# Values projected with the tokens on the partitions and moved by DMA, their weighting moved from VectorE to GpSimd, and the input normalisation moved ahead

## The reference, cut to what matters

```python
def layer(x, txt):                      # 32 images of 3x96x96, 32 texts of 32x256
    z = layernorm(patches(x)) @ W_proj  # 36 patches of 768 values -> 256
    h = concat([cls, layernorm(z)]) + pos
    h = concat([h, txt], axis=1)        # 32 x 69 tokens x 256
    n = layernorm(h)
    q, k, v = n @ q_w + q_b, n @ k_w + k_b, n @ v_w + v_b      # 16 heads of 64
    attn = softmax(q @ k.T / 8)                                # 69 x 69 each
    h = h + concat(attn @ v) @ l_w.T + l_b
    return h + moe(layernorm(h))        # top 2 of 8 experts, each 256 -> 1024 -> 256, capacity 690
```

## Time and profile before

| | |
|---|---|
| time, median of 3 runs | 701.84 us (701.57 to 702.82) |
| profiled execution: time, span | 701.51 us, 699.7 us |
| busy PE / DVE / ACT / POOL | 681.5 / 505.0 / 296.1 / 276.6 us |
| stage A until about | 48 us |
| stage B, first `context` to last | 58.58 to 397.34 us |
| finishing the routing, first fetch | until 422.7 us |
| stage D until about | 692.7 us for PE |

### The profile page before, as it was taken

The page is one execution under the profiler, slowest core; times in us unless marked ns, Lnnn a source line. Parts: engine busy times, 40 slices in busy tenths (PEclk is TensorE's granted clock), DMA queues, the critical chain, the costliest instruction groups (busy, mean ns, idle before and its releaser), DMA issues.

```text
span 699.7 us, 16960 instructions
## 1 busy us (share of the span) xinstructions
PE 681.5 (97%) x6671; PEld 647.9 (93%) x6671; DVE 505.0 (72%) x1157; ACT 296.1 (42%) x655; POOL 276.6 (40%) x294
## 2 busy tenths in 40 slices
PE   8989999999999999999999999999999999999995
PEld 6878899998999999999999998999999999999995
DVE  6978877988979889798877756765757474837471
ACT  4454545445454454544544225333424251615130
POOL 4654010130401304012030453766666666565715
PEclk9999999999999999999999999999999999999999
DMA  8831000000000000000000412544444544534202
GB/s 268 263 95 27 1 2 18 14 16 9 19 18 12 17 9 19 18 11 17 11 19 18 139 46 89 127 82 136 75 125 84 114 93 95 104 85 102 24 7 30
DMA packets 51579, 42.99 MB, mean 61 GB/s; under 512 B 25493, under 2 KB 45139, under 8 KB 51515
## 3 DMA queue, kind: packets, MB, share of 16 engines
q1 hardware_dynamic: 20171, 27.85, 12.8%
q0 software_dynamic: 29168, 11.61, 10.4%
q10 hardware_dynamic: 2176, 2.64, 1.3%
HBM read 32.76 MB, written 10.25 MB: 61 GB/s over the span
## 4 chain that ended last, share of the span: by engine, by line
PE 73%; DVE 14%; issue 4%; DMA 2%; POOL 2%; SPq 2%; ACT 1%; POOLq 0%; DVEq 0%; ACTq 0%
PE pair L1540 11%; PE pair L1542 11%; PE pair L1541 11%; PE lone L1540 8%; PE lone L1541 8%; PE lone L1542 8%; PE pair L1658 4%; PE ct_ps L1668 4%; PE vt_ps L1645 3%; DVE vals L1147 2%; DVE zsum L1137 2%; DVE top L1128 2%; SPq L439 2%; DVE expo L1131 1%; POOL out L792 1%
## 5 line engine op out<-in xcount | busy, mean ns | idle before, releaser
L792 POOL DMA_INDIRECT out<-yrow,held x48 | 100.9, 2102 | 62.7 <-DVE yrow L1501 46.2
L1023 ACT ACTIVATE act_f<-pair 128x348 f32<-128x348 f32 (+1 forms) x120 | 48.9, 457 | 92.0 <-PE pair L1542 87.2
L773 POOL DMA_INDIRECT held<-token_rows,found_ix x48 | 69.5, 1448 | 33.6 <-issue 22.0
L1540 PE MATMUL pair<-xe_hi,fc_hi 128*128 128x348 f32 (+1 forms) x256 | 82.1, 321 | 0.6 <-DVE xe_lo L1471 0.3
L1542 PE MATMUL pair<-xe_hi,fc_lo 128*128 128x348 f32 (+1 forms) x256 | 82.2, 321 | 0.0
L1541 PE MATMUL pair<-xe_lo,fc_hi 128*128 128x348 f32 (+1 forms) x256 | 82.2, 321 | 0.0
L1540 PE MATMUL lone<-pj_hi,act_hi 128*116 128x256 f32 (+1 forms) x256 | 72.2, 282 | 0.0
L1542 PE MATMUL lone<-pj_hi,act_lo 128*116 128x256 f32 (+1 forms) x256 | 71.9, 281 | 0.0
L1541 PE MATMUL lone<-pj_lo,act_hi 128*116 128x256 f32 (+1 forms) x256 | 71.8, 280 | 0.0
L856 ACT ACTIVATE expo<-expo 69x552 f32<-69x552 f32 x64 | 42.5, 664 | 55.4 <-DVE expo L1131 54.6
L842 ACT ACTIVATE qkv<-pair,bq_sb 128x276 f32<-128x276 f32 x97 | 47.1, 485 | 33.8 <-PE pair L1542 33.3
(11 more groups left out here) (259 smaller groups left out, 2018.8 us busy)
## 6 DMA issues: line engine op xcount, KB each, us to landing
raw_fc<-c_fc SPq DMA_DIRECT2D x8, 1024.0 KB
raw_pj<-c_proj SPq DMA_DIRECT2D x8, 1024.0 KB
raw<-w_qkv SPq DMA_DIRECT2D x6, 512.0 KB, 9.0
out<-h SPq DMA_DIRECT2D x8, 276.0 KB
token_rows<-sent POOLq DMA_DIRECT2D x7, 285.7 KB, 7.0
raw<-patches SPq DMA_DIRECT2D x3, 384.0 KB, 5.0
raw<-patches ACTq DMA_DIRECT2D x3, 384.0 KB, 6.9
raw<-w_l ACTq DMA_DIRECT2D x1, 1024.0 KB, 6.8
```

Source lines behind the costliest of these rows:

```text
L773: pool.indirect_dma_start(xg[p][0:n, t, :], None, x2_dram, bass.IndirectOffsetOnAxis(ap=found_ix[p][0:n, t:t + 1].bitcast(U32), axis=0), b ...
L792: pool.indirect_dma_start(out, bass.IndirectOffsetOnAxis(ap=xg[p][0:n, t, D:D + 1].bitcast(U32), axis=0), yrow[p][0:n, t, :], None, bounds ...
L1023: gelu = act.activation(act_f[f % 2][:, a:b], pair[f % 2][:, h, 0:b - a], ACT.Gelu)
L1540: pe.matmul(dst, l_hi, r_hi, start=(first and n == 0), stop=False)
```

## The change

What was the v part of `project_qkv` becomes `project_values(n)`: the 92 tokens of a tile are the output rows and 512 value columns (half of the 16 heads) the moving side, so the result already has tokens on partitions and nothing has to be transposed. There are 6 such tiles for a group (3 token tiles by 2 halves), 48 in all, of 6 matmuls each. Tiles 0 to 2 come before the first unit, one in each unit 0 to 8 after that, and then one in each of the units 2 to 7, for the following group. `turn_values` is gone, and its bank is the fifth of the shared ones.

DVE adds the bias and writes each tile to one of three staging buffers (`put_values`), one unit later. Because a token tile has 92 rows and a sequence 69, SP moves each tile in two DMAs from the staging buffer to `value_rows`, where each sequence begins at partition 0 (`move_values`). POOL multiplies them by `zinv` (`weigh_values`, two instructions for each unit), except for the very last unit, which DVE does. DVE's `reciprocal` waits for POOL's use of the buffer two units back.

`norm_in` is done two groups ahead in unit 5 (for group 1 in unit 0 as before), `norm_in_end` in unit 0, and `turn_x` and `low_xT` in unit 1 (for group 1 in unit 2), so that the value tiles of the next group can begin in unit 2.

```diff
-BANKS = 4
+BANKS = 5
+def turning(g):
+    return 1 if g else 2
+def value_tiles(m):
+    g, u = divmod(m, UNITS)
+    n = VTILES * g
+    tiles = [n + VTILES + u - 2] if u >= 2 else []
+    if m <= UNITS:
+        tiles = [TPG + m]
+    return [i for i in tiles if i < VTILES * GROUPS]
@@ SP, behind move_rows(PT - 1) @@
+            def move_values(n):
+                g, k = divmod(n, VTILES)
+                h, t = divmod(k, TPG)
+                if g >= 1 and t == 0:
+                    sp.wait_ge(s_val, UNITS * (g - 1) + (h + 1) * UNITS // 2)
+                if n == TPG:
+                    sp.wait_ge(s_wq_lo, 6)
+                    sp.wait_ge(s_wq_lo2, 6)
+                bank, nth = USE[("value", n, 0)]
+                sp.wait_ge(s_free[bank], nth)
+                for b, n0, r, _, m in VALUE_RUNS[t]:
+                    sp.dma_start(value_rows[h][n0:n0 + m, b // 2, b % 2, :], value_tile[t][r:r + m, :])\
+                        .then_inc(s_moved[t], 16)
+            for n in range(TPG):
+                move_values(n)
+            for g in range(GROUPS):
+                for n in range(VTILES * g + TPG, VTILES * (g + 1)):
+                    move_values(n)
+                if g >= 1:
+                    store_h(g - 1)
+                if g + 1 < GROUPS:
+                    for n in range(VTILES * (g + 1), VTILES * (g + 1) + TPG):
+                        move_values(n)
@@ POOL @@
+            def weigh_values(m):
+                g, u = divmod(m, UNITS)
+                h, n = divmod(u, UNITS // 2)
+                if n == 0:
+                    for p in range(TPG):
+                        pool.wait_ge(s_moved[p], landed(VTILES * g + (h + 1) * TPG, p))
+                pool.wait_ge(s_zi, m + 1)
+                if m >= 2:
+                    pool.wait_ge(s_ctx, m - 1)
+                v = value_rows[h][:, :, :, n * 128:(n + 1) * 128]
+                for k in range(2):
+                    done = pool.tensor_tensor(
+                        vals[u % 2][:, 4 * k:4 * k + 4, :].rearrange("s (b e) d -> s b e d", e=2),
+                        v[:, k, :, :].rearrange("s b (e d) -> s b e d", e=2),
+                        zinv[u % 2][:, :].rearrange("s (e k b) -> s k b e", e=2, k=2)[:, k, :, :].unsqueeze(3)
+                        .broadcast_to([SEQ, 2, 2, HD]), ALU.mult)
+                done.then_inc(s_val, 1)
             def stage_b(g):
+                weigh_values(UNITS * g)
+                if g == 0:
+                    root_in(st, 1)
+                    low_wq(5)
                 if g >= 2:
-                    spread(Step(g), -2)
-                if g + 1 < GROUPS:
-                    root_in(Step(g), 1)
+                    spread(st, -2)
+                weigh_values(UNITS * g + 1)
+                weigh_values(UNITS * g + 2)
+                if before:
+                    root_mid(st, -1)
+                weigh_values(UNITS * g + 3)
...
                 if g + 2 < GROUPS:
+                    add_positions(st, 2)
+                weigh_values(UNITS * g + 4)
+                weigh_values(UNITS * g + 5)
+                if g + 2 < GROUPS:
+                    root_in(st, 2)
+                weigh_values(UNITS * g + 6)
+                if before:
+                    widen(st, -1)
+                if more:
+                    weigh_values(UNITS * g + 7)
+                if before:
+                    weigh(st, -1)
+                    store_x2(st, -1)
@@ DVE @@
+                wait(dve, s_val, st, lambda i: UNITS * i + u - 1)
+                dve.reciprocal(zinv[u % 2][:, :], zsum[:, :]).then_inc(s_zi, 1)
+            def put_values(n):
+                g, k = divmod(n, VTILES)
+                h, t = divmod(k, TPG)
+                bank, nth = USE[("value", n, 0)]
+                dve.wait_ge(s_full[bank], nth)
+                if n >= TPG:
+                    dve.wait_ge(s_moved[t], landed(n - 1, t))
+                dve.tensor_tensor(value_tile[t], shared[bank][0:TR, 0:VCOLS], bv_sb[:, h * VCOLS:(h + 1) * VCOLS], ALU.add)\
+                    .then_inc(s_free[bank], 1)
...
-                if u == 5 and more:
-                    low_xT(st, 1)
                 sum_exp(st, u)
+                if m == ALL - 1:
+                    weigh_last_values()
                 if m >= 1:
                     low_ctx(Step((m - 1) // UNITS), (m - 1) % UNITS)
-                weigh_values(st, u)
                 if m + 1 < ALL:
                     take_max(Step((m + 1) // UNITS), (m + 1) % UNITS)
+                if m >= 1:
+                    for n in value_tiles(m - 1):
+                        put_values(n)
+                if u == turning(g) and more:
+                    low_xT(st, 1)
...
-                if u == 1 and more:
+                if u == turning(g) - 1 and more:
                     norm_in_end(st, 1)
...
+                if u == 5 and g + 2 < GROUPS:
+                    norm_in(st, 2)
@@ PE @@
+            def project_values(n):
...
+                r, w = slice(t * TR, (t + 1) * TR), value_columns(h)
+                x_hi, x_lo = xT_hi[g % 2], xT_lo[g % 2]
+                three(shared[bank][0:TR, 0:VCOLS], [(x_hi[:, k, r], x_lo[:, k, r], wq_hi[:, k, w], wq_lo[:, k, w])
+                                                    for k in range(KD)]).then_inc(s_full[bank], 1)
...
+            for n in range(TPG):
+                project_values(n)
             for m in range(LEAD):
-                for j in range(3):
+                if m:
+                    score(0)
+                for j in range(2):
                     project_qkv(m, j)
...
-                turn_values(m)
...
+                if u == turning(g) and more:
+                    turn_x(st, 1)
...
-                if blocks:
-                    project_qkv(m + LEAD, 2)
+                for n in value_tiles(m):
+                    project_values(n)
...
-                if u == 4 and more:
-                    turn_x(st, 1)
```

More of the change, by code:

```diff
@@ L119, with pair_columns, value_columns, landed @@
 TEXT_RUNS = runs(1 + NPATCH, NTXT)
+VALUE_RUNS = [[run for run in runs(0, SEQ) if run[3] == t] for t in range(TPG)]
+def pair_columns(u, j):
+    at = PAIR_PIECES[u // 2] * PIECE + (2 * (u % 2) + j) * 128
+    return slice(at, at + 128)
+def value_columns(h):
+    return slice(VALUE_PIECES[h] * PIECE, (VALUE_PIECES[h] + 1) * PIECE)
+def landed(n, p):
+    return 16 * sum(len(VALUE_RUNS[i % TPG]) for i in range(p, n, TPG))
 class Step:
@@ L165, in bank_uses @@
     last = GROUPS - 1
-    order = [("xt", 0, c) for c in range(KD)] + [("qkv", m, j) for m in range(LEAD) for j in range(3)]
+    order = [("xt", 0, c) for c in range(KD)]
+    order += [("value", n, 0) for n in range(TPG)] + [("qkv", m, j) for m in range(LEAD) for j in range(2)]
     for m in range(ALL):
@@ L180, in unit_uses @@
         uses += {4: [("x2t", g - 1, c) for c in range(KD)], 5: [("logit", g - 1, 0)]}.get(u, [])
+    if g + 1 < GROUPS and u == turning(g):
+        uses += [("xt", g + 1, c) for c in range(KD)]
     if m == ALL - 2:
         uses += [("proj", g, c) for c in range(KD)]
-    uses += blocks[:2]
+    uses += blocks
     if g >= 1 and u == 2:
         uses += [("ytr", g - 1, n) for n in range(2)]
-    uses += blocks[2:]
+    uses += [("value", n, 0) for n in value_tiles(m)]
     if g >= 1 and u == (7 if g + 1 < GROUPS else 6):
@@ L194, in unit_uses @@
         uses += [("mean", 0, 0)]
-    if g + 1 < GROUPS and u == 4:
-        uses += [("xt", g + 1, c) for c in range(KD)]
     return uses
 def program(nc, patches, txt, ln1_g, ln1_b, w_proj, b_proj, ln2_g, ln2_b, cls, pos,
-            w_qkv, b_qkv, w_l, b_l, w_g, c_fc, c_proj, ident_in, id_parts, out):
+            w_qkv, b_qkv, b_v, w_l, b_l, w_g, c_fc, c_proj, ident_in, id_parts, out):
     USE = bank_uses()
@@ L275, in program @@
         wl_lo = sb("wl_lo", [128, PAIRS, D], F32R, bmem)
-        qkv = [sb(f"qkv{i}", [128, 3, GT], F32, bmem) for i in range(RING)]
+        qk_all = sb("qk_all", [128, RING, 2, GT], F32, bmem)
+        qkv = [qk_all[:, i, :, :] for i in range(RING)]
         with ExitStack() as rmem:
@@ L647, in root_mid, with widen @@
                 pool.tensor_copy(sent[:, :, D:D + 1].bitcast(I32), ids[:, t, :]).then_inc(s_ids, 1)
+            def widen(st, shift):
+                wait(pool, s_pick, st, lambda i: PICKS * (i + shift + 1))
+                pool.tensor_tensor(gap[:, :], best[:, 1, :], best[:, 0, :], ALU.subtract).then_inc(s_gap, 1)
+            def weigh_values(m):
[15 more added lines that the diff above has]
+                done.then_inc(s_val, 1)
             def weigh(st, shift):
@@ L653, in before @@
                     wait(pool, s_prob, st, lambda i: 6 * (i + shift) + n)
-                wait(pool, s_pick, st, lambda i: PICKS * (i + shift + 1))
-                pool.tensor_tensor(gap[:, :], best[:, 1, :], best[:, 0, :], ALU.subtract).then_inc(s_gap, 1)
                 wait(pool, s_egap, st, lambda i: i + shift + 1)
@@ L937, in unit @@
```

(23 more changed lines are left out.)

116 lines of the change are left out of this document (66 added, 50 removed).

## The result

The changed kernel takes **728.1 us** (median of 4 runs, 726.87 to 729.79) against 701.71 us (701.15 to 702.82) for the kernel before: ratio 1.0367, 95% interval 1.0345 to 1.0390. It is slower by 3.7%, where 696.5 us was forecast and 703 was the upper end. Its profiled span is 725.3 us, 25.6 more than before. The `context` rows of PE (line 1816 now) say where they lie.

A forecast was written before the change was run, and what follows sets the result against it. PE was taken to set the pace, with DVE close behind. 14.0 + 2.2 - 0.9 - 16.2 - 5.7 + 1.3 = -5.3 against the profiled 701.51 gave 696.2, and 0.33 to the median 696.5; range 689 to 703.

The forecast's parts named there:

- The start, +14.0: First `context` at 72.6 instead of 58.6 us, because unit 0's weighting waits for six moves late in SP's queue; bounds 12 and 17.
- landing as the last rows did, 65.64 - 64.27 = 1.4: At the start, the first value moves' data arrive 1.4 us behind their last issue, like the last row moves.
- Group 0, -0.9: Group 0 with the head of group 1: 38.6 us plus about 0.7 of waits, against 40.23; bounds -1.6 and +3.
- rival (e): Start costs more: 2 KB row moves at 1.6 us an issue, 701.4, or group 0 repeats the wait, 705; chance 0.09.
- The clock, +2.2: PE's granted clock falls while PE idles 10 us at the start, and coming back costs 2.2 us; bounds 0 and 3.
- Steady groups, -2.7 each: PE per group: transposes and v projections removed, value tiles added, net -2.3, and 0.4 of waits returned; six times, -16.2.
- Does DVE keep up?: Steady groups: DVE loses 1.2 us a group; unit 5 takes 6.2 against PE's 5.3, yet unit 6 stays covered.
- Rival (d): DVE loses time to the port shared with POOL, 0.6 us holds in unit 5 or 6: 703.5 or 699; chance 0.12.
- Last group and tail: Last group, without value tiles or transposes, -5.7, bounds -4 and -7; tail with later POOL work +1.3.
- (c): POOL's weighting becomes the loop's limit; at 1.9 us an instruction 707; chance 0.12, mostly slower.
- (f): A PE slot of 512 columns costs only 0.160, as one of 348: 20 us less, 680; chance 0.03.
- (b): The start hardly waits, as SP issues the moves faster or earlier: 687; chance 0.12.

The follow-up runs named there:

- run 2: Changed kernel with the six first value moves issued ahead of the last two patches' row moves instead of behind them; 718.69 us, ratio 1.0254.
- run 3: Changed kernel with each value move split into a multiple of 16 rows and the rest; 721.75 us, ratio 1.0296.
- run 1: Changed kernel without the six moves of value tiles 0 to 2 and every wait on them (output partly wrong); 710.19 us, ratio 1.0123.
- run 10: Changed kernel with the edits of run 2, run 3, run 4 and run 5, and ACT issuing value tile 2's four moves; 691.74 us, ratio 0.9861.
- runs 8 and 9: Changed kernel with the edits of run 2, run 3, run 4 and run 5, 696.37 us; same plus 24 spare PE matmuls before first `context`, 695.30 us.
- run 4: Changed kernel with DVE putting the value tile away ahead of the next unit's maximum and subtraction; 714.46 us, ratio 1.0188.
- run 5: Changed kernel with POOL's `add_positions` behind the weighting of unit 4 instead of ahead of it; 724.67 us, ratio 1.0322.
- Run 12: Changed kernel with the edits of run 2, run 3, run 4 and run 5, value weighting moved from POOL to DVE; 736.82 us, ratio 1.0510.

## Why the prediction was wrong

**The start, +14.0: the landing was mis-sized.** The queue's part was right (issues end at 68.65; 0.67 each instead of 0.78). The step that failed is "landing as the last rows did, 65.64 - 64.27 = 1.4": it took a time from moves of 14 to 36 rows of 1 KB for moves of 69, 46 and 23 rows of 2 KB, and added 0.6 for the size. I counted bytes and issues, not the engines over which a move is spread: by the small packets a move of 36 rows ran on twelve engines (24 for two of them, from 64.3 to 65.9 us), one of 69, 46 or 23 on three, two or one. The landing was 10.5 us, here and in run 2, and 1.5 in run 3, with each move cut in two. PE's own part of the start was also taken 1.1 us too small (run 1), which counts only once the wait is gone.

**Group 0, -0.9: rival (e)'s wait was real.** The same landing, put into the 0.7 of waits at the second half, failed here again. The second half's first weighting waited for the moves (6.44 us of POOL behind `DMA raw<-raw`), and the two intervals there are 7.21 and 5.91 us instead of 4.4: 4.3 us, of which 2.8 are the wait and 1.5 the clock, granted at 0.71 behind it. Run 3 brings them to 4.99 and 4.39. In run 10, where this and the start's wait are gone, group 0 is at -0.6, near the forecast.

**The clock, +2.2: right in size for the start**, 2.4 us between runs 8 and 9, but the second fall in group 0, 1.5 us more, was not in the sum. That the size came right is in part luck: it was priced from the run's first matmuls "at the low level", and the profile of the kernel before reads 1.00 for 0 to 8 us. Their pace, 0.22 us for 256 columns, is that of the low level all the same: at 0.50 a slot of 276 columns takes 0.23 (83.14 to 83.37 us of the changed kernel).

**Steady groups, -2.7 each: two steps failed.** The larger is an omission. "Does DVE keep up?" looked only at whether PE's next `score` finds its operands; I never followed a bank from the value tile to its next use. It costs 44.00 - 41.87 = 2.1 us a group, of which the order on DVE is 1.6 (run 4) and the shared port 0.6 (run 5). Rival (d) named this port, but priced it by holds of 0.6 us on instructions of unit 5 or 6, less DVE's slack ahead of `score`, not in unit 4, where PE waits for a bank. The smaller is a size. The slot of 512 columns takes 0.23, as taken. But the last slot ahead of `context` takes longer than its fellows: 238.53 to 238.85 is 0.32 instead of 0.23, and 126.84 to 127.06 is 0.22 instead of 0.127 where a block of 276 columns comes last. In the kernel before, the transposes stood there, and the slot ahead of them was no longer, 0.13:

```profile
229.45 0.29 PE L1542 MATMUL lone<-ctx,wl_lo 128*128 128x276 f32 x1
229.58 0.60 PE L1645 MATMUL vt_ps<-ident,qkv 128*69 128x128 f32 x4
230.11 0.28 PE L1668 MATMUL ct_ps<-expo,vals 69*64 69x69 f32 x2
```

So removing them returns 0.56 - 0.1, 8 x 0.1 = 0.8 a group less: -2.7 + 0.8 = -1.9, and the best kernels show 41.87 - 43.81 = -1.9. That it closes so well is in part luck: where nothing waits the transposes take 0.53, not the 0.56 of the earlier trace rows, and unit by unit the returned waits are more than the 0.4 of the sum in two intervals (4.64 to 4.41 and 4.86 to 4.79, which a value tile alone would have lengthened by 0.2 each), while another loses 0.2 again (5.16 to 5.07, although `turn_x` with its 0.5 left it).

**Last group and tail**: -4.5 for -5.7, +0.7 for +1.3, both within their bounds.

**The rivals.** (c) is refuted: an instruction of the weighting takes 0.620 us in the mean of 126 (75.6 us), and from 100 to 360 us of run 10 the view of PE's waits is empty. Run 12 shows the opposite: without POOL, and in the order tried there, the change loses 40 us. (f) is refuted by the same slot of 0.23. The figure of 131 ns in the Trainium skill, "TensorE: Matmul & The Clock Gate", "Back-to-back issue gap", does not hold here either. (b) never applied. (e) was right in kind and too small: it priced a costlier issue (701.4) or the repeated wait (705), each alone, and no longer landing. The sum with the measured sizes closes: +21.9 + 6.3 + 1.2 - 4.5 + 0.7 = +25.6.

What stays open: which DMA engines carried the moves. That all shares begin on the same one is inferred from the rows under way at a time, three, then two, then one, not read from an engine's number. Why the clock fell at the end of stage A in some kernels and not in others is open too.

## What to carry to other kernels

Before a transfer is put on a path, factor its rows: a move of 69, 46 or 23 rows ran on three, two or one engine, and cutting it into a multiple of 16 and a rest turned 10.5 us of landing into 1.5, for six issues more. When a value passes through a ring of buffers, follow each buffer to its next user through the heaviest unit: a consumer that is fast enough on average still stalls PE if it stands two instructions too late in its queue. A change can be right in its core (here 16 us of gain from group 1 on, 11.6 + 4.5) and lose through its seams, so look at the seams one by one before giving it up.
